# ScalarE adds the bias of projected q and k while copying them out of PSUM; VectorE rotates them from SBUF

## The reference

```
q = proj(query, Wq, bq)          # x @ Wq.T + bq, 16 heads of 16
k = proj(key, Wk, bk)
q = q * cos + _rotate_half(q) * sin
k = k * cos + _rotate_half(k) * sin
scores = einsum('bhqd,bhkd->bhqk', q, k) / sqrt(16)   # |i - j| <= 50, then softmax
out = einsum('bhqk,bhkd->bhqd', softmax(scores), v)
x = x + tanh(g_xattn) * (out @ Wo.T + bo)
x = x + tanh(g_ffn) * ffn(layernorm(x))               # after all batches
```

## Time and profile before

| what | value |
|---|---|
| median of 3 runs | 1427.61 us (1423.87 to 1428.71) |
| the profiled execution | 1429.06 us, of it a span of 1427.3 us |
| PE busy over the span | 1286.9 us (90%) |
| DVE busy | 1213.0 us (85%) |
| ACT busy | 835.7 us (59%) |
| POOL busy | 585.8 us (41%) |
| mean granted TensorE clock | 0.969 |

### The profile page before, as it was taken

One profiled execution on the slowest core, in us unless ns is written; L12 is line 12 of the kernel. 1 busy time (PEld: TensorE's weight loads), 2 busy tenths in 40 slices (PEclk: granted clock), 3 DMA queues, 4 the chain that ended last, 5 costly groups with the idle time before them and its releaser, 6 DMA issues. The chain is left out here.

```text
span 1427.3 us, 27869 instructions
## 1 busy us (share of the span) xinstructions
PE 1286.9 (90%) x8992; PEld 837.0 (59%) x8992; DVE 1213.0 (85%) x3572; ACT 835.7 (59%) x1336; POOL 585.8 (41%) x1392
## 2 busy tenths in 40 slices
PE   3378999999999999999999886999899979987998
PEld 2256777767777777777777552444343334436887
DVE  4678898989899898989898744999799989997886
ACT  2225565656565666666566544665577679993332
POOL 1127777777777777777777650000000000000000
PEclk9969999999999999999999997999999999997999
DMA  3175656565656566665656400222455546556674
GB/s 111 41 152 122 162 133 158 135 157 138 153 142 149 142 150 146 147 152 147 146 148 148 103 31 30 110 102 96 147 185 186 177 166 198 191 180 198 228 242 162
DMA packets 132369, 207.27 MB, mean 145 GB/s; under 512 B 11159, under 2 KB 97050, under 8 KB 126106
## 3 DMA queue, kind: packets, MB, share of 16 engines
q1 hardware_dynamic: 132250, 205.86, 51.6%
HBM read 125.60 MB, written 79.69 MB: 144 GB/s over the span
## 5 line engine op out<-in xcount | busy, mean ns | idle before, releaser
L705 DVE CUSTOM_DVE_ANT_0 psum<-psum,band 128x178 f32<-128x178 f32 x1024 | 318.2, 371 | 40.8 <-PE psum L833 40.5
L589 ACT ACTIVATE probs<-psum 128x356 f32<-128x356 f32 x512 | 209.8, 463 | 232.4 <-PE psum L850 232.2
L520 POOL TENSOR_SCALAR_AFFINE_SELECT probs<-probs 128x154 f32<-128x154 f32 (+1 forms) x512 | 213.7, 426 | 169.1 <-ACT probs L589 164.2
L1008 PE MATMUL psum<-xnT,w_upT 128*128 (+1 forms) x1152 | 261.7, 385 | 18.9 <-DVE maxima L1232 8.8
L1008 PEld LDWEIGHTS psum<-xnT,w_upT 128*128 128x128 f16 x1152 | 109.9, 99 | 170.5 <-issue 33.4
L875 PE MATMUL psum<-probs,V 128*32 128x178 f32 x2048 | 206.8, 321 | 2.0 <-POOL probs L529 1.9
L529 POOL TENSOR_SCALAR_AFFINE_SELECT probs<-probs 128x254 f32<-128x254 f32 (+1 forms) x512 | 189.1, 393 | 0.0
L833 PE MATMUL psum<-k_stack,q_stack 96*128 96x178 bf16 x1024 | 129.9, 244 | 20.2 <-issue 7.3
L1608 PE MATMUL psum<-w_downT,xnT 128*128 128x256 f16 x1152 | 128.5, 276 | 15.9 <-DVE xnT L1558 15.9
L705 DVE DVE_READ_ACCUMULATOR2_ANT smax<- 128x1 f32 x1024 | 141.4, 138 | 0.0
L1008 PE MATMUL psum<-xnT,w_gateT 128*128 (+1 forms) x576 | 127.3, 385 | 8.8 <-DVE xnT L1081 8.8
(11 more groups left out here) (190 smaller groups left out, 2296.2 us busy)
## 6 DMA issues: line engine op xcount, KB each, us to landing
k_parts_scratch<-k_parts SPq DMA_DIRECT2D x32, 384.0 KB, 2.6
q_parts_scratch<-q_parts SPq DMA_DIRECT2D x32, 384.0 KB, 2.6
k_stack<-k_parts_scratch SPq DMA_DIRECT2D x32, 384.0 KB, 5.1
q_stack<-q_parts_scratch SPq DMA_DIRECT2D x32, 384.0 KB, 5.0
gate_scratch<-g_stage SPq DMA_DIRECT2D x16, 768.0 KB, 3.3
g_in<-gate_scratch SPq DMA_DIRECT2D x16, 768.0 KB, 4.6
sig_scratch<-w_gateT SPq DMA_DIRECT2D x32, 384.0 KB, 2.4
sig_again<-sig_scratch SPq DMA_DIRECT2D x32, 384.0 KB, 3.4
```

The lines of the kernel that those rows point to most:

```text
L520: nc.gpsimd.affine_select(out=t[:, :, 0:n], in_=t[:, :, 0:n], pattern=[[0, 2], [1, n]], compare_op=ALU.is_ge, fill=0.0, base=WINDOW - off, ...
L589: nc.scalar.activation(ring_tile(probs, b, pair, c)[:].rearrange("p e j -> p (e j)"), scoreT_bank[c][:, 0:2 * SPAN], ACT.Exp, scale=DK ** ...
L705: ins = nc.vector.tensor_tensor_reduce(out=mine, in0=mine, in1=keep["band"][:, t, :], scale=1.0, scalar=-3e38, op0=ALU.add, op1=ALU.max, a ...
L1008: last = nc.tensor.matmul(bank[:], weights[wp][:, c * I + f * P:c * I + (f + 1) * P], x_parts[:, c, bass.ds(j * (2 * TILE) + xp * TILE, TI ...
```

## The change

ACT gets a new step `add_bias`: two instructions per tensor of 256 columns each, which read the projection from PSUM, add the bias and write it to `by_cos` in SBUF. It stands at the head of slot 2 for k and at the head of slot 3 for q. `rope` no longer reads PSUM: it waits for both of these (`biased`), multiplies all 512 columns by sin with the halves swapped into `by_sin`, waits for that product, and multiplies `by_cos` by cos in place. `rotate` on POOL now waits for two products. PE may write the two banks again once ACT, and no longer DVE, has read them.

```
+            def add_bias(b, n, bank):
+                if not b.real:
+                    return
+                reached(act, projected[n], b, 1, 1)
+
+                reached(act, rest_ready[n], b.before(1), 1, 1)
+                for half in range(2):
+                    at = half * S
+                    k = 2 * "qk".index(n) + half
+                    nc.scalar.activation(by_cos[n][:, at:at + S], bank[:, at:at + S], ACT.Identity,
+                                         bias=keep["qk_bias"][:, k:k + 1]).then_inc(biased[n], 1)
...
+                    if slot == 2:
+                        add_bias(b0, "k", bank_b)
                     if slot == 3:
+                        add_bias(b0, "q", bank_a)
                         high(b0, "k")
...
-            def rope(b, n, bank):
+            def rope(b, n):
...
-                reached(dve, projected[n], b, 1, 1)
+                reached(dve, biased[n], b, 2, 2)
...
-                bias = keep["qk_bias"][:, 2 * "qk".index(n):2 * "qk".index(n) + 2]
-                for half in range(2):
-                    at = half * S
-                    nc.vector.scalar_tensor_tensor(by_cos[n][:, at:at + S], bank[:, at:at + S], bias[:, half:half + 1],
-                                                   keep["cos"][:], ALU.add, ALU.mult).then_inc(multiplied[n], 1)
-                    nc.vector.scalar_tensor_tensor(by_sin[n][:, S - at:2 * S - at], bank[:, at:at + S], bias[:, half:half + 1],
-                                                   keep["sin"][:, S - at:2 * S - at], ALU.add, ALU.mult)\
-                        .then_inc(multiplied[n], 1)
+                halves = [P, 2, S]
+                straight = by_cos[n][:].rearrange("p (a t) -> p a t", a=2)
+                nc.vector.tensor_tensor(by_sin[n][:].rearrange("p (a t) -> p a t", a=2), straight[:, ::-1, :],
+                                        keep["sin"][:].rearrange("p (a t) -> p a t", a=2), ALU.mult)\
+                    .then_inc(multiplied[n], 1)
+                reached(dve, multiplied[n], b, 2, 1)
+                nc.vector.tensor_tensor(straight, straight, keep["cos"][:].unsqueeze(1).to_broadcast(halves), ALU.mult)\
+                    .then_inc(multiplied[n], 1)
...
-                        reached(pe, multiplied["k"], b0, 4, 4)
+                        reached(pe, biased["k"], b0, 2, 2)
```

More of the change, by code:

```diff
@@ L361, in attention @@
         x_normed = sem("x_normed")
+        biased = {n: sem(f"{n}_biased") for n in "qk"}
         multiplied = {n: sem(f"{n}_multiplied") for n in "qk"}
@@ L506, in rotate @@
                     return
-                reached(pool, multiplied[n], b, 4, 4)
+                reached(pool, multiplied[n], b, 2, 2)
                 nc.gpsimd.tensor_tensor(rot[n][:], by_cos[n][:], by_sin[n][:], ALU.add).then_inc(rotated[n], 1)
@@ L761, in steps @@
                     if slot == 2:
-                        rope(b0, "k", bank_b)
+                        rope(b0, "k")
                         divide(b3, 0)
@@ L765, in steps @@
                         shift_parts(b2, 1)
-                        rope(b0, "q", bank_a)
+                        rope(b0, "q")
                     if slot == 4:
@@ L912, in steps @@
                         else:
-                            reached(pe, multiplied["q"], b0.before(1), 4, 4)
+                            reached(pe, biased["q"], b0.before(1), 2, 2)
                         transpose4(bank_a, c_in[:].rearrange("p t d -> p (t d)")).then_inc(c_transposed, 1)
@@ L931, in steps @@
                         if b0.real:
-                            reached(pe, multiplied["q"], b0, 4, 4)
+                            reached(pe, biased["q"], b0, 2, 2)
                         elif b4.real:
```

## The result

| | before | after |
|---|---|---|
| median | 1428.16 us (4 runs) | 1509.17 us (4 runs, 1507.21 to 1511.76) |
| span of the profiled execution | 1427.3 us | 1507.3 us |

The ratio is 1.0574 (95% interval 1.0546 to 1.0601): the change makes the kernel slower by 81 us.

What follows compares the result with a forecast made beforehand. PE was taken to set the pace (97% busy), with DVE close behind. 29 passes of 2.02 us plus 3 us for the start gave 61.6 us, so 1489 us was predicted, with 80% from 1457 to 1518.

Steps and rivals of the forecast that it cites:

- The place of the bias on ACT: The bias of k stands behind the exponentials of slot 1, so DVE starts rotating k at 409.29, not 407.08.
- the term of +2.21: Later start of DVE's rotation of k, waiting for ACT's bias: +2.21 us a pass (2.00 to 2.42).
- The products: DVE's two products replacing four take 1.30 us for k and 1.50 for q, against 1.57 before.
- The terms -0.27 and -0.07: DVE time saved a pass by two products instead of four: -0.27 us for k, -0.07 us for q.
- The shift: DVE's shift, with a two-SBUF-input instruction, runs beside POOL's late cut: +0.15 us a pass, bounds 0 and 0.84.
- No new wait for q: The bias of q is ready at 412.47, before DVE arrives at 413.09, so it adds 0.
- nothing absorbed: From slot 4 PE runs its own list, so the delay stays; rival of absorption: 5% for some 1443, 4% within 0.3%.
- nothing lost in the feed-forward: The feed-forward is untouched by the change and adds no time.
- the sum for one pass: Scores of slot 4 start 2.02 us later (2.21 - 0.27 + 0.15 - 0.07), so the 23.52 us pass grows by that.
- PE's waits: PE waits 1 to 2 us for DVE's maxima ahead of the scores of slots 3 and 4.
- Faster: Rival: ACT does the bias in idle time ahead of its exponentials and DVE's relief counts, about 1416 us; chance 3%.
- The sum of 3.7 us for that rival: Rival: POOL holds DVE's two-input products or the shift, 3.7 us a pass, 1538 us; chance 8% for 1518 and above.

Runs made afterwards that it cites:

- e6_fill: The changed kernel, with PE doing the two matmuls of one head a second time in the weighting of slots 2 and 3: 1487.97 us.
- e3_early: The changed kernel, with the bias of k moved ahead of the exponentials of slot 1 and that of q ahead of those of slot 2: 1455.07 us.
- e5_delay_0: The kernel before, with 2.0 us of idle DVE work per pass in slot 0, behind the residual and ahead of the maxima: 1462.70 us.
- e2_q_only: The changed kernel, with k put back to four products from PSUM, so only q is rotated the new way: 1474.35 us.
- e4_delay_k: The kernel before, with 2.0 us of idle DVE work per pass right behind the wait for the projection of k: 1532.60 us.
- e1_k_only: The changed kernel, with q put back to four products from PSUM, so only k is rotated the new way: 1539.37 us.
- e8_four_sbuf: The changed kernel, with four DVE products of 256 columns from SBUF in place of two of 512: 1542.39 us.

## Why the prediction was right, and where it was off

- *The place of the bias on ACT.* It starts at 339.16, right behind the exponentials, and DVE 2.22 us after the projection: the term of +2.21 measured +2.18. The two bias instructions take 0.84 us for a pair (I took 0.87).
- *The products.* 1.33 us for k (I had 1.30) and 1.32 for q (I had 1.50, with POOL's cut beside the first). The terms -0.27 and -0.07 were -0.24 and -0.25. I had the cut at the wrong tensor: by my own starts (409.29 against the addition at 409.58) it was not over when the products of k began. In the quiet pass it runs from 339.70 to 340.91, beside the first product of k and the start of the second; they kept their 0.69 us, and the cut took 1.21 us where the same two instructions take 0.69 elsewhere, which delays nobody here. Beside the product of q, at 344.03, the cut was all but over (343.40 to 344.09). That -0.27 came out nearly right although the cut stood there was luck.
- *The shift.* I added 0.15 to its second instruction; it took 0.30 more, and most of it was on the first (0.44 against 0.20).
- *No new wait for q, nothing absorbed, nothing lost in the feed-forward.* All as forecast. The sum of 2.02 us a pass measured 2.01, in part by luck: the shift cost 0.15 us more than I had, the products of q 0.18 less. 28 such passes (I had 29) with 3.8 us for the start (I had 3) give some 60 us, which e6_fill confirms (1487.97 us; my number was 1489).
- *The step that fell short* is in the sum for one pass: "The pass becomes 23.52 + 2.02 us", taken for all passes alike. I had noted the full clock of the stage and never asked what PE's new waits would do to it. The term that is missing is the passes with a lowered clock, 21 us by e6_fill. The range held it only because it was wide for other reasons; that the time lies inside is luck in this part.
- *PE's waits.* I had the scores of slots 3 and 4 wait 1 to 2 us for DVE's maxima. In the usual quiet pass it is 0.39 + 0.20 + 0.44 + 0.27 = 1.30 us. The wait of 0.51 us for the shift, between the two, was not among what I named.
- *The rivals.* "Faster" would have needed the bias ahead of the exponentials; e3_early built that, and it is still 1.9% slower than before, while the bias on ACT still puts some 0.9 us between PE's result and the rotation. For the 1416 us of that rival I took 12 us off without a working; the terms named there add up to 31. DVE's products were not held by POOL in the changed kernel's quiet passes, while its remainder of k was in e3_early. The sum of 3.7 us for that rival counts 0.23 a tensor, where its condition, 0.90 for each product, would give more.

## What to carry to other kernels

When work moves to an engine with idle time, read what stands ahead of it in that engine's list and what that waits for: ACT was 62% busy and still began the bias 1.3 us late, because its idle time lay before an instruction that came first. An engine's lower busy time (DVE 12 us less) is worth nothing when it starts later at the place where the bounding engine waits for it. And where the bounding engine is PE, add to the delay what PE's clock may do with the new gaps.

## What the runs showed of the hardware

Five waits of 0.20 to 0.51 us, 1.8 us in all, stand in slots 3 and 4 of the usual pass of 25.5 us, none of them long. With them the granted clock fell in 10 of 28 passes, which took 1.5 to 3.2 us longer each; with most of them filled by matmuls (e6_fill) it stayed at 1.00 over 130:780. In all ten it fell between 9.5 and 11.5 us after the projection of k had begun, which is at the waits of slot 4 (9.8 to 10.8 us) or right behind them. The pass that begins at 386.96 shows it, before, in and after the lowered stretch:

```profile
393.00:396.00 3.00, 1.91 (x20) 0.91 (x18) 2.90 (x14) 1.92 (x6) 2.14 (x5) 1.00 0.67 231
397.00:403.00 6.00, 5.71 (x23) 3.80 (x24) 4.81 (x21) 3.25 (x7) 5.48 (x12) 0.50 0.19 58
404.00:408.00 4.00, 4.00 (x44) 3.00 (x43) 3.44 (x20) 3.02 (x7) 2.56 (x6) 1.00 0.02 4
```

The clock is at its upper level while PE stands idle for more than a third of the time in slot 3, then at 1.2 GHz (0.50) although PE is busy nearly throughout, then full again. The pass at 361.43, with the same waits, kept the full clock; why one and not the other stays open.

The length of the quiet pass does not order the kernels. Over 130:780 the clock was 1.00 in e3_early and e5_delay_0 (24.42 and 24.73 us), 0.98 in e2_q_only (24.77), 0.96 in the changed kernel and 1.00 in e6_fill (25.53 both), 0.94 in e4_delay_k and e1_k_only, 0.93 in e8_four_sbuf (25.92). In e1_k_only and e4_delay_k, whose quiet passes (25.77; 25.55 to 25.79) are at most 0.3 us longer than those of the changed kernel, nearly every pass had a lowered stretch and took 27.1 to 27.4 us, and the medians are 30 and 23 us above that of the changed kernel. Why these two fell so regularly and the changed kernel only now and then stays open.
